# Seeding score banks with the mask: one column tile or two, by ScalarE alone or with VectorE

## The chip, the core and the metric

The kernel runs on one core of one Trainium2 chip. The metric is the time of one execution on the device in microseconds (us); the number compared is the median of several runs. A separate, profiled execution gives the trace. PE is TensorE's matmul part, PEld its weight loads, DVE is VectorE, ACT is ScalarE, POOL is GpSimd and SP is the SyncE queue that starts most DMAs. PSUM is the memory that matmuls write to, in eight banks of 128x512 f32.

## The reference, cut to what matters

The input x is 8 batches of 512 tokens with 256 features. Four layers follow one another, each added to x: a masked attention with 16 heads of 16 features, a mixture of 8 experts of which each token uses 2, and two linear maps. The change touches the attention:

```python
scores = jnp.einsum('bhsd,bhtd->bhst', q, k) * scale
scores = jnp.where(mask[None, None, :, :], -jnp.inf, scores)
attn = jax.nn.softmax(scores, axis=-1)
out = jnp.einsum('bhst,bhtd->bhsd', attn, v)
```

After it come an output projection, an RMS norm with gain and shift, the gate that picks two experts per token, and the experts.

## The kernel before, in words

The kernel first writes a list of steps, `order`, on the host; each engine then walks this one list and emits its own part of every step. Every engine therefore works in the order of the list, and waits are semaphores between engines.

**Groups and tiles.** Attention goes by groups: 4 heads of one batch, so 4 groups per batch and `GROUPS` = 32. The loop of `attention_order` runs over iterations i = 0 to 34, and inside over k = 0 to 3. One (i, k) is called a tile below. A tile holds, for n = 0 to 3, one `row` step and one `col` step. A `row` step multiplies queries by keys for 128 queries of group i (L1170), and DVE adds the mask and finds the maximum over the keys (L1643). These maxima are shared out again as extra rows of the queries (`split_maxima`, `maxima_rows`, and a small DMA, L984). A `col` step two iterations later computes the transposed scores of group i-2 for 128 keys, kt = k, of head hh = n, with the maximum already taken off (L1184). The mask must be added to them too. By default PE does that with a second matmul into the same bank, the identity times the mask (L1188). ACT then takes the exponential into `pt` (L1369).

**Seeds.** Where the list allows, the mask is in the bank before the scores are: ACT copies the mask there (L1375), and PE's score matmul adds onto it, without L1188. This is a seed. Before the change there is one per tile from group 1 on: 31 groups x 4 tiles = 124. `seed_after` says behind which exponential ACT makes it: two `col` steps ahead of the one that uses it (`SEED_AHEAD`). ACT must wait until the bank's last user has been read out.

**The ring.** Rows, columns and all side matmuls take seven banks in turn (`RING`). The user seven places earlier must have been read out before a bank is used again. With rows and columns alternating, the bank of a column was last that of a row. One side matmul in between makes it that of a column three places earlier.

**Side work.** `weigh` (the value products, L1203) stands in tiles with even k behind n = 2 and takes two key tiles at once. The other PE work of a batch waits in a list `todo`: 4 `project` (queries and keys of the next batch, L1147), 4 `project_v` (L1156) with 3 `stack` steps (DMAs that load the stacked parts of queries and keys), 4 `project_o` (L1221) and the `chain`. `work_off` takes one step of it at the end of each tile; it takes a `stack` step along with what stands before it. A chain is the norm, gate and routing of one batch as a generator: each of its yields is one n of a tile. It holds `scale` (DVE, L1692), `normalised` (POOL), the transposes `turn_x1`, squares (ACT, L1316), the gate, and `scatter` (POOL, indirect DMAs, L1980). Chains of later batches wait for earlier ones. In tiles of iterations 32 and 33 there are no rows, only columns.

**Weights for the experts.** Along the attention POOL splits expert weights into two parts in 64 chunks: SP fetches a chunk (L995), POOL splits it (L1879, L1881), SP stores it (L1000). `attention_over` lets the expert phase begin when the last chunk is stored. On SP's queue the last chunk's fetch stands behind `fetch_rows` (L1057), which waits for the scatters of batches 0 to 5.

**The expert phase** follows from about 615 us on, with matmuls at L1101. The diff does not touch its steps, but what is left of the last two chains runs in it.

Of the kernel before, what the change touches and what calls it, by code (L numbers as in the profile page):

```python
# [27 lines left out]
GROUPS = B * NG  # L28
# [19 lines left out]
SEED_AHEAD = 2  # L48
SHIFTS = 2
# [80 lines left out]
def chain(b, out):  # L130
# [10 lines left out]
    for st in range(ST):  # L141
        out.append(("scale", b, st))
        yield
# [7 lines left out]
    for st in range(ST):  # L151
        out.append(("square_x1", b, st))
        yield
# [95 lines left out]
def attention_order(out):  # L249
# [14 lines left out]
    def work_off():  # L264
        step = todo.pop(0)
        if step[0] == "chain":
            chains.append(chain(step[1], out))
        else:
            out.append(step)
            if step[0] == "project":  # L270
                rests.append(("rest",) + step[1:])
        if todo and todo[0][0] == "stack":
            work_off()
# [15 lines left out]
    for i in range(GROUPS + 3):  # L289
# [7 lines left out]
        for k in range(ST):  # L297
# [3 lines left out]
            for n in range(GH):  # L301
# [14 lines left out]
                if i * ST + k in FIRST_PROJECTS and n == 1 and i < 2:  # L316
                    work_off()
                if n == (3 if i < 2 else 0) and rests:
                    step = rests.pop(0)
                    out.append(step)  # L320
                    parted.append(("part",) + step[1:])
# [32 lines left out]
            for _ in range(2 if len(todo) > 12 else 1):  # L354
                if todo and i >= 2:
                    work_off()
# [83 lines left out]
def _build(nc, ctx, d, out):  # L440
# [323 lines left out]
    seed_after = {}  # L764
    for gi in range(1, GROUPS):
        for kt in range(ST):
            for hh in ((3, 2, 1, 0), (0, 1, 2, 3))[kt % 2]:
                place = col_place[gi, kt, hh]
                user = ring_before(("col", gi, kt, hh))
                if user[0] == "row" or user[0] == "col" and col_place[user[1:]] <= place - SEED_AHEAD:  # L770
                    seed_after[cols_at[place - SEED_AHEAD]] = gi, kt, hh
                    break
    seeded = signal("seeded", [seed_after[at] for at in cols_at if at in seed_after])
    project_place = {at: n for n, at in enumerate(projects)}
# [314 lines left out]
    def tensor_program(engine):  # L1089
# [49 lines left out]
        for step in order:  # L1139
# [32 lines left out]
            elif name == "col":  # L1172
# [3 lines left out]
                seed = (gi, kt, hh) in seeded.value  # L1176
                if seed:
                    pe.wait_ge(*seeded.at((gi, kt, hh)))
                else:
# [300 lines left out]
    def vector_program(engine):  # L1480
# [117 lines left out]
        for step in order:  # L1598
# [35 lines left out]
            elif name == "row":  # L1634
# [6 lines left out]
                if gi >= 2:  # L1641
                    dve.wait_ge(*max_split.at((gi - 2,)))
                V.tensor_tensor_reduce(junk[n % 2][:, :], ring_bank(step)[0][:, :], mneg[:, 0, st, :], 1.0, FLOOR, ALU.add, ALU.max,  # L1643
                                       rowmax[gi % 2][:, hh, st:st + 1]).then_inc(max_found.sem, 1)
            elif name == "split_maxima":
# [397 lines left out]
```

## Time and profile before

| what | value |
|---|---|
| median of 3 runs | 1162.13 us (1159.18 to 1162.16) |
| the profiled execution, its own time | 1156.71 us |
| its span from first to last instruction | 1154.8 us |
| mean granted TensorE clock | 0.991 of full speed |
| PE busy / DVE / ACT / POOL | 97% / 67% / 68% / 44% |

Busy time of PE is the union of matmul records whose ends are modelled: a 512-column matmul has a record of 0.38 us, but the next one starts 0.22 us later. Where PE is never short of work, the distance between starts is therefore its cost. All times in the trace are counted from the first instruction.

### The profile page before, as it was taken

The page shows a single profiled execution, that of the slowest core. Times are in us where ns is not written, and L with a number is a line of the kernel's source. Part 1 is how long each engine was busy: PE and PEld are TensorE (multiplying, and loading weights), DVE is VectorE, ACT ScalarE, POOL GpSimd, SP SyncE. Part 2 cuts the span into 40 slices and gives each one's busy share as a digit, 9 for nine tenths or more (in the row PEclk, how much of TensorE's full clock was granted, in tenths as well). Part 3 has the DMA queues.
Part 4 walks back from the last instruction along what each step waited for, and adds up shares of the span by engine and source line. Part 5 has one row for each costly group of instructions (what it writes and reads, how often), then busy time and mean ns, then how long its engine had stood idle before and what let it go on. Part 6 is the DMA issues. An engine that isn't in the chain of part 4 may idle for free.

```text
span 1154.8 us, 23346 instructions
## 1 busy us (share of the span) xinstructions
PE 1115.1 (97%) x7466; PEld 779.2 (67%) x7520; DVE 776.1 (67%) x2265; ACT 790.7 (68%) x1752; POOL 511.7 (44%) x837
## 2 busy tenths in 40 slices
PE   8899999999999999998988999999999999999988
PEld 5333434435344353443438989999999999999968
DVE  5877778787887878877745435356555555668647
ACT  2478778787787877866794656656566656666645
POOL 7424135584755837557552465354222222222210
PEclk8999999999999999998999999999999999999999
DMA  8765738367383663844737588846566666723536
GB/s 209 211 191 189 223 101 254 121 224 232 117 276 123 221 209 120 269 139 127 262 106 271 136 291 304 262 122 144 161 188 201 202 193 193 215 49 69 165 91 219
DMA packets 101616, 213.64 MB, mean 185 GB/s; under 512 B 10917, under 2 KB 71341, under 8 KB 93046
## 3 DMA queue, kind: packets, MB, share of 16 engines
q1 hardware_dynamic: 86038, 192.42, 51.3%
q0 software_dynamic: 14304, 18.69, 9.0%
q10 hardware_dynamic: 1152, 1.05, 0.4%
q8 instruction: 59, 0.97, 0.4%
q14 instruction: 63, 0.52, 0.1%
HBM read 239.28 MB, written 74.29 MB: 272 GB/s over the span
## 4 chain that ended last, share of the span: by engine, by line
PE 45%; POOL 2%; DMA 2%; DVE 2%; issue 1%; ACT 1%; SPq 1%; POOLq 0%; ACTq 0%
PE bank L1101 38%; PE bank L1261 1%; PE bank L1116 1%; DMA x<-yout,rows 1%; PE bank L1130 1%; PE bank L1203 1%; PE bank L1221 1%; POOL routed L1980 1%; DMA routed<-xw,idx 0%; PE bank L1295 0%; PE bank L1184 0%; PE bank L1170 0%; PE bank L1241 0%; DMA w_parts<-in_W 0%; POOL run L862 0%
## 5 line engine op out<-in xcount | busy, mean ns | idle before, releaser
L1643 DVE CUSTOM_DVE_ANT_0 junk<-bank,mneg 128x512 bf16<-128x512 f32 x512 | 332.5, 683 | 105.4 <-PE bank L1170 104.9
L1369 ACT ACTIVATE pt<-bank 128x512 f32<-128x512 f32 x512 | 300.9, 595 | 65.5 <-PE bank L1184 31.9
L1990 POOL DMA_INDIRECT x<-yout,rows x78 | 122.5, 1570 | 291.2 <-ACT yout L1453 231.1
L1101 PE MATMUL bank<-hid,w 128*128 128x256 f32 x1872 | 244.7, 287 | 3.9 <-DVE hid L1791 3.9
L1101 PEld LDWEIGHTS bank<-hid,w 128*128 128x128 f32 x1872 | 231.4, 191 | 5.6 <-issue 4.3
L1791 DVE TENSOR_TENSOR hid<-full,hid 128x256 fp32r<-128x256 f32 x312 | 133.1, 430 | 139.1 <-ACT full L1448 137.9
L1443 ACT ACTIVATE hid<-bank,biases 128x256 fp32r<-128x256 f32 x312 | 149.9, 480 | 93.2 <-PE bank L1101 91.3
L1448 ACT ACTIVATE full<-bank,biases 128x256 f32<-128x256 f32 x312 | 149.2, 478 | 0.0
L1188 PE MATMUL bank<-mneg,identb 128*128 128x512 bf16 x332 | 126.4, 381 | 0.0
L1203 PE MATMUL bank<-pt,vaug 128*17 128x512 f32 x1024 | 124.0, 602 | 1.4 <-DVE turned L1670 0.5
L1101 PE MATMUL bank<-w,hid 128*128 128x256 f32 x936 | 121.9, 283 | 1.5 <-DVE hid L1791 1.5
L1101 PE MATMUL bank<-rowsT,w 128*128 128x256 f32 x936 | 122.9, 284 | 0.2 <-DMA w<-split_weights 0.2
L1101 PEld LDWEIGHTS bank<-rowsT,w 128*128 128x128 f32 x936 | 116.0, 190 | 0.9 <-DVE rowsT L1782 0.7
L1101 PEld LDWEIGHTS bank<-w,hid 128*128 128x128 f32 x936 | 115.1, 190 | 1.7 <-issue 1.7
L1170 PE MATMUL bank<-stacks 96*128 96x512 bf16 x256 | 95.7, 389 | 8.0 <-DVE rest L1608 2.9
L1453 ACT ACTIVATE yout<-yout,rows 128x256 f32<-128x256 f32 x78 | 39.3, 508 | 92.5 <-DVE yout L1797 92.5
L1184 PE MATMUL bank<-qst,kst 98*128 98x512 bf16 x256 | 97.0, 382 | 5.5 <-DVE rowmax L1643 4.5
L1170 PE MATMUL bank<-kst,qst 96*128 96x512 bf16 x256 | 98.0, 383 | 2.4 <-DVE rowmax L1643 1.1
L1184 PE MATMUL bank<-stacks 98*128 98x512 bf16 x256 | 97.3, 380 | 2.7 <-DVE rowmax L1643 1.4
L1881 POOL TENSOR_TENSOR w_parts<-w_parts 128x512 fp32r<-128x512 f32 x64 | 81.6, 1274 | 5.2
L1375 ACT ACTIVATE bank<-mneg 128x512 f32<-128x512 bf16 x124 | 74.2, 598 | 8.5 <-DVE rowmax L1643 8.1
L1980 POOL DMA_INDIRECT routed<-xw,idx x64 | 64.3, 1005 | 17.1 <-issue 13.5
(184 smaller groups left out, 1455.0 us busy)
## 6 DMA issues: line engine op xcount, KB each, us to landing
w<-split_weights SPq DMA_DIRECT2D x80, 1024.0 KB
w<-split_weights SPq DMA_DIRECT2D x40, 2048.0 KB
split_weights<-w_parts SPq DMA_DIRECT2D x64, 512.0 KB, 3.8
w_parts<-in_W SPq DMA_DIRECT2D x64, 256.0 KB, 4.6
split_parts<-parts SPq DMA_DIRECT2D x28, 384.0 KB, 2.6
rows<-routed SPq DMA_DIRECT2D x39, 258.0 KB, 3.7
stacks<-split_parts SPq DMA_DIRECT2D x36, 256.0 KB, 5.5
qst<-split_parts SPq DMA_DIRECT2D x24, 256.0 KB, 5.2
```

The source lines that it names most:

```text
L1101: product = T.matmul(ps, w[p], x[q], start=(k == 0 and n == 0), stop=(k == len(weights) - 1 and n == 2))
L1170: T.matmul(ps[:, :], qst[b % 2][0:KQ, h, st * P:(st + 1) * P], kst[b % 2][0:KQ, h, :], start=True, stop=True).then_inc(row_scored.sem, 1)
L1184: product = T.matmul(ps[:, :], kst[b % 2][0:KQ + SHIFTS, h, kt * P:(kt + 1) * P], qst[b % 2][0:KQ + SHIFTS, h, :], start=not seed, stop=li ...
L1188: product = T.matmul(ps[:, :], identb[:, :], mneg[:, 1, kt, :], start=False, stop=True)
L1203: product = T.matmul(bank[5][32 * hh:32 * hh + D + 1, :], vaug[b % 2][:, kt, h, :], pt[col_place[gi, kt, hh] % len(pt)][:, :], start=(kt = ...
L1369: A.activation(pt[n % len(pt)][:, :], ps[:, :], ACT.Exp, scale=float(D) ** -0.5).then_inc(exped.sem, 1)
L1443: A.activation((hid1, hid2)[n - 1][j % 2][0][:, m, :], ps[:, 0:TW], ACT.Relu, bias=biases[j % NS][:, column:column + 1])
L1448: A.activation(full[place % len(full)][:, :], ps[:, 0:TW], ACT.Relu, bias=biases[j % NS][:, column:column + 1]).then_inc(rectified.sem, 1)
L1643: V.tensor_tensor_reduce(junk[n % 2][:, :], ring_bank(step)[0][:, :], mneg[:, 0, st, :], 1.0, FLOOR, ALU.add, ALU.max, rowmax[gi % 2][:, h ...
L1791: V.tensor_tensor(lo, h[:, :], hi.bitcast(F32), ALU.subtract).then_inc(hidden_low.sem, 1)
L1881: G.tensor_tensor(w_parts[n][:, 1], w_parts[n][:, 1].bitcast(F32), w_parts[n][:, 0].bitcast(F32), ALU.subtract).then_inc(w_low.sem, 1)
L1990: G.indirect_dma_start(x2_dram, bass.IndirectOffsetOnAxis(ap=rows[j % NS][:, tt, E + 1:E + 2].bitcast(U32), axis=0), yout[j % NY][:, tt], ...
```

## The change

It has two parts. The first makes two seeds per tile. In tiles with even kt, and in all tiles of the last two groups, ACT makes both. In tiles with odd kt of groups 1 to 29, ACT makes the first and DVE one more: behind the row maximum of the third row step before the column (`ROWS_AHEAD` = 3), if the bank's last user is far enough back. The order in which heads are tried changes too.

The second moves side work. From iteration 2 on, `work_off` is called only in tiles with odd k (those without `weigh`): at the tile's end, and also behind n = 1 unless the next step is a `project`. From iteration 30 on the end of every tile still calls it. A chain is now taken together with the step before it, so it begins earlier. For batches 0 to 4 the steps of `scale` and `square_x1` stand two yields apart instead of one.

```diff
+ROWS_AHEAD = 3
...
     for st in range(ST):
         out.append(("scale", b, st))
-        yield
+        for _ in range(2 if b < KNOWN - 1 else 1):
+            yield
...
     for st in range(ST):
         out.append(("square_x1", b, st))
-        yield
+        for _ in range(2 if b < KNOWN - 1 else 1):
+            yield
...
-        if todo and todo[0][0] == "stack":
+        if todo and todo[0][0] in ("stack", "chain"):
             work_off()
...
+                if k % 2 and n == 1 and i >= 2 and todo and todo[0][0] != "project":
+                    work_off()
...
-            for _ in range(2 if len(todo) > 12 else 1):
-                if todo and i >= 2:
-                    work_off()
+            if todo and i >= 2 and (k % 2 or i >= GROUPS - 2):
+                work_off()
...
-    seed_after = {}
+    rows_before, n = {}, 0
+    for step in order:
+        n += step[0] == "row"
+        if step[0] == "col":
+            rows_before[step[1:]] = n
+
+    def early(user, at):
+        if user[0] == "row":
+            return row_place[user[1:]] <= rows_before[at] - ROWS_AHEAD
+        return user[0] == "col" and col_place[user[1:]] <= col_place[at] - ROWS_AHEAD
+
+    seed_after, seed_behind = {}, {}
     for gi in range(1, GROUPS):
         for kt in range(ST):
-            for hh in ((3, 2, 1, 0), (0, 1, 2, 3))[kt % 2]:
-                place = col_place[gi, kt, hh]
+            by_vector = kt % 2 and gi < GROUPS - 2
+            free = []
+            for hh in ((3, 1, 2, 0), (0, 2, 1, 3))[kt % 2]:
                 user = ring_before(("col", gi, kt, hh))
-                if user[0] == "row" or user[0] == "col" and col_place[user[1:]] <= place - SEED_AHEAD:
-                    seed_after[cols_at[place - SEED_AHEAD]] = gi, kt, hh
-                    break
+                if user[0] == "row" or user[0] == "col" and col_place[user[1:]] <= col_place[gi, kt, hh] - SEED_AHEAD:
+                    free.append((gi, kt, hh))
+            for at in free[:1 if by_vector else 2]:
+                seed_after[cols_at[col_place[at] - SEED_AHEAD]] = at
+            for at in [at for at in free[1:] if by_vector and early(ring_before(("col", *at)), at)][:1]:
+                seed_behind[rows_at[rows_before[at] - ROWS_AHEAD]] = at
...
+                after = seed_behind.get((gi, hh, st))
+                if after:
+                    ps, freed = ring_bank(("col", *after))
+                    dve.wait_ge(masks_made, MASKS)
+                    dve.wait_ge(*freed)
+                    V.tensor_copy(ps[:, :], mneg[:, 1, after[1], :]).then_inc(seeded_too.sem, 1)
```

In the diff's last part, on DVE, the copy follows the row maximum at once. PE waits for `seeded_too` before the column that uses it.

## Rows read from the trace of the kernel before

**Rows 1.** The stages: us, busy time (instructions) of each engine, clock, DMA.
```profile
215.77:288.15 72.38, 71.86 (x391) 31.71 (x397) 58.98 (x172) 57.65 (x121) 45.71 (x92) 1.00 0.62 194
506.04:577.69 71.65, 65.34 (x361) 25.91 (x366) 56.01 (x171) 51.40 (x110) 45.13 (x99) 0.95 0.52 181
577.69:601.50 23.81, 20.80 (x125) 7.21 (x127) 11.23 (x41) 21.85 (x49) 16.33 (x34) 1.00 0.37 114
```

**Rows 2.** Waits of PE between 143.41 and 506.04 us, all of them.
```profile
PE bank L1170 <- DVE rowmax L1643: 0.8, 2, 0.4
```

**Rows 3.** Timeline of PE from tile (13, 0) to (13, 2): start, us.
```profile
236.55 0.38 PE L1170 MATMUL bank<-kst,qst 96*128 96x512 bf16 x1
...
240.89 0.38 PE L1170 MATMUL bank<-kst,qst 96*128 96x512 bf16 x1
...
242.20 0.38 PE L1184 MATMUL bank<-stacks 98*128 98x512 bf16 x1
...
243.52 0.38 PE L1170 MATMUL bank<-kst,qst 96*128 96x512 bf16 x1
```

**Rows 4.** Timeline of DVE in the same tile.
```profile
240.88 0.69 DVE L1643 CUSTOM_DVE_ANT_0 junk<-bank,mneg 128x512 bf16<-128x512 f32 x1 [0.16 <-PE bank L1170]
...
241.49 0.69 DVE L1643 CUSTOM_DVE_ANT_0 junk<-bank,mneg 128x512 bf16<-128x512 f32 x1
```

**Rows 5.** DVE groups by shape, whole span: us, mean ns of one.
```profile
L1692 DVE SCALAR_TENSOR_TENSOR osb<-osb,ssq,gain_shift 128x256 f32<-128x256 f32 x32 | 23.5, 736 | 1.3 <-POOL ssq L862 1.3
...
L1653 DVE CAST m<-rowmax 128x16 bf16<-128x16 f32 x32 | 12.1, 378 | 1.3 <-POOL below L1831 1.2
...
L1615 DVE MEMSET bank<- 128x512 f32 x1 | 0.5, 485 | 0.1
```

**Rows 6.** DVE groups by shape, 215.77 to 288.15 us.
```profile
L1655 DVE TENSOR_TENSOR m<-rowmax,m 128x16 bf16<-128x16 f32 x4 | 2.6, 651 | 0.1
```

**Rows 7.** Timeline of PE, tile (22, 1).
```profile
401.87 0.39 PE L1170 MATMUL bank<-kst,qst 96*128 96x512 bf16 x1 [0.40 <-DVE rowmax L1643]
```

**Rows 8.** Timeline of all engines around tile (30, 0).
```profile
537.97 1.56 DVE L1692 SCALAR_TENSOR_TENSOR osb<-osb,ssq,gain_shift 128x256 f32<-128x256 f32 x1
537.99 1.26 POOL L1881 TENSOR_TENSOR w_parts<-w_parts 128x512 fp32r<-128x512 f32 x1
...
540.20 0.61 PE L1184 MATMUL bank<-qst,kst 98*128 98x512 bf16 x1 [1.27 <-DVE rowmax L1643]
```

**Rows 9.** The same tile as a stage, columns as in rows 1.
```profile
537.14:547.06 9.92, 8.07 (x32) 1.96 (x31) 6.77 (x18) 3.65 (x7) 7.04 (x9) 0.66 0.54 159
```

**Rows 10.** ACT groups by shape, 577.69 to 601.50 us.
```profile
L1369 ACT ACTIVATE pt<-bank 128x512 f32<-128x512 f32 x31 | 16.9, 606 | 2.9 <-PE bank L1188 2.4 <-PE bank L1184 0.5
L1375 ACT ACTIVATE bank<-mneg 128x512 f32<-128x512 bf16 x8 | 4.9, 619 | 0.2 <-DVE rowmax L1643 0.2
L1316 ACT ACTIVATE squared<-osb 128x256 bf16<-128x256 f32 x4 | 1.7, 418 | 0.0
L1316 ACT ACTIVATION_READ_ACCUMULATOR squared<-osb 128x1 f32 x4 | 0.8, 203 | 0.0
```

**Rows 11.** The chain that ended last, end of attention: start, us.
```profile
591.91 2.43 DMA routed<-xw,idx
...
605.54 4.04 DMA w_parts<-in_W
...
611.87 2.62 DMA split_weights<-w_parts
```

**Rows 12.** SP's timeline there.
```profile
585.70 0.62 SPq L984 DMA_DIRECT2D qst<-mrow  x1
595.45 0.42 SPq L1057 DMA_DIRECT2D rows<-routed  x1
```

**Rows 13.** Waits of PE between 506.04 and 614.74 us: us in total, times, longest.
```profile
PE bank L1184 <- DVE rowmax L1643: 5.5, 6, 1.4
PE bank L1261 <- DMA split_weights<-w_parts: 4.6, 1, 4.6
```

More of the change, by code:

```diff
@@ L762, in ring_before @@
         return ring_users[n] if n >= 0 else None
-    seed_after = {}
+    rows_before, n = {}, 0
[8 more added lines that the diff above has]
+    seed_after, seed_behind = {}, {}
     for gi in range(1, GROUPS):
         for kt in range(ST):
-            for hh in ((3, 2, 1, 0), (0, 1, 2, 3))[kt % 2]:
-                place = col_place[gi, kt, hh]
+            by_vector = kt % 2 and gi < GROUPS - 2
+            free = []
+            for hh in ((3, 1, 2, 0), (0, 2, 1, 3))[kt % 2]:
                 user = ring_before(("col", gi, kt, hh))
-                if user[0] == "row" or user[0] == "col" and col_place[user[1:]] <= place - SEED_AHEAD:
-                    seed_after[cols_at[place - SEED_AHEAD]] = gi, kt, hh
-                    break
+                if user[0] == "row" or user[0] == "col" and col_place[user[1:]] <= col_place[gi, kt, hh] - SEED_AHEAD:
[4 more added lines that the diff above has]
+                seed_behind[rows_at[rows_before[at] - ROWS_AHEAD]] = at
     seeded = signal("seeded", [seed_after[at] for at in cols_at if at in seed_after])
+    seeded_too = signal("seeded_too", [seed_behind[at] for at in rows_at if at in seed_behind])
     project_place = {at: n for n, at in enumerate(projects)}
@@ L1175, in tensor_program @@
                 ps, freed = ring_bank(step)
-                seed = (gi, kt, hh) in seeded.value
-                if seed:
+                seed = (gi, kt, hh) in seeded.value or (gi, kt, hh) in seeded_too.value
+                if (gi, kt, hh) in seeded.value:
                     pe.wait_ge(*seeded.at((gi, kt, hh)))
+                elif seed:
+                    pe.wait_ge(*seeded_too.at((gi, kt, hh)))
                 else:
```

## The prediction

> **What bounds the kernel now.** I read the stages first, because PE's 97% is a union of modelled records and says little. In a batch period of attention the engines other than PE have slack: of 72.38 us DVE is busy 58.98 and ACT 57.65 [rows 1]. Then the waits: in 362.6 us of steady attention PE waits 0.8 us in all [rows 2]. The timeline shows what that means. Six 512-column matmuls lie between the starts at 240.89 and 242.20, so one costs 1.31 / 6 = 0.218 us, and a whole tile without side work takes 2.63 us [rows 3]. Iterations 4 to 27 are bound by PE alone, and a matmul taken from PE there gives 0.218 us, if nothing else becomes late. At the end it is different. In iterations 28 to 31 (506.04 to 577.69) PE waits for DVE and its clock falls for a while; in 32 and 33 ACT is busy 21.85 of 23.81 us [rows 1]. Then PE waits 4.6 us for the last chunk of expert weights [rows 13].
>
> **Term 1, the masks.** The old rule makes 124 seeds. By ring arithmetic two banks of four are nearly always allowed: the new rule makes 62 x 2 (even kt), 58 + 8 (odd kt) by ACT, and 58 by DVE. 248 seeds take 124 more mask matmuls off PE. Eight stand in iterations 32 and 33, where PE isn't the bound. 116 x 0.218 = 25.3 us come off. This is all of the gain that the edit aims at, 2.2% of the time.
>
> **Term 2, the wait for DVE's seeds.** ACT's second seed in an even tile is behind a column after which PE still has the value products or the next side work; I cost it at nothing in iterations 4 to 31. ACT gets 8 x 0.6 = 4.8 us more per batch and stays at 62.5 of some 72; if its cover goes, a wait of that length shows up. DVE's seed is closer. Take an odd tile without a step behind n = 1, row 0 starting at t = 0. PE issues row 0, column 0 (seeded by ACT), row 1, column 1, its mask, row 2, and wants column 2 at 6 x 0.218 = 1.31. That column is DVE's (order 0, 2, 1, 3: the first free is ACT's, the next DVE's), and its copy is behind row 0. In tile (13, 1) the row 0 started on PE at 240.89 and its maximum on DVE at 241.49, 0.60 later, held by the maximum before; two maxima start 0.61 apart [rows 3, 4]. So the copy starts at 1.21. Its length is on no row. Nearest below is DVE's memset of a bank, 0.485, which reads nothing; nearest above is the maximum itself, 0.69, which reads a bank and the mask [rows 4, 5]. I take 0.65, near the top, as it reads a source. The copy ends at 1.86, PE goes on at about 1.92 (0.06 for the semaphore, an estimate), so it stands 0.61 us. Between the bounds it is 0.45 to 0.65. Queued behind PE's wait are all its later matmuls; nothing later in the tile gives the time back.
>
> Where a side step stands behind n = 1 (0.87 us for a value or output tile), column 2 is wanted at 2.18, and the wait is gone. So I count tiles: the four `project` of a batch are at the head in the odd tiles of iterations i with i mod 4 = 0 and 1, which have no step behind n = 1: 24 tiles for six batches. Iterations 28 and 29 have no side work: 4. (30, 1), (31, 1), (31, 3): 3. Iteration 3: 2. That is 33 of 58 odd tiles: 33 x 0.61 = 20.1 us, and the other 25 at nothing. Four masks per group give 0.87 us; two such tiles take back 1.2. (Bounds: 33 x 0.45 = 14.9 to 33 x 0.65 = 21.5.)
>
> **Term 3, DVE late.** The wait assumes that DVE is level with PE. `scale` steps now fall on calls 12, 14, 16 and 18 of a chain: two in tile (12, 3), two in (13, 0) (and every four iterations). In (13, 0) DVE has four maxima at 0.61, `split_maxima` at about 0.35 + 0.65, a `rest` at 0.6, and two `scale` at 0.74: 5.5 us [rows 4 to 6], where PE needs 4.34 [rows 3] less one mask, 4.12. Something of this is hidden by the value products. I carry 1.0 us into (13, 1), a tile of term 2, whose wait becomes 1.6. Five chains: +5.0. Before, the four `scale` stood in one tile and cost PE one such wait per chain, as in tile (22, 1), 0.40 [rows 7]; x 5 this goes: -2.0.
>
> **Term 4, iterations 28 to 31.** Chain 5 now begins at (28, 0) and not at (28, 3). Its four `scale` stay one n apart. Before, one took 1.56 us beside a POOL split of 1.26, PE waited 1.27 at once, and the clock was at half right after it (0.61 for a record of 0.38) [rows 8]; tile (30, 0) took 9.92 us at clock 0.66 [rows 9], some 5 more than the 4.34 of [rows 3] with its transpose. The same pile-up comes three tiles earlier behind a bare tile. I take -3 (that the clock holds), with +3 as the other end.
>
> **Term 5, iterations 32 and 33.** Eight tiles get one more ACT copy. ACT starts an exponential every 0.61 us there and is the bound: 8 x 0.61 = +4.9. But chain 6 now begins in iteration 31, so four squares of 0.418 + 0.203 leave this stretch: -2.5 [rows 10]. Net +2.4.
>
> **Term 6, the last chunk.** SP issues `fetch_rows` at 595.45, right after the scatters of chain 5 land (591.91 + 2.43). Its `mrow` DMA before it went at 585.70, so it stood for over 9 us. The chunk's fetch (605.54), split and store (to 614.5) hang on that [rows 11, 12]. Chain 5 ends 13 calls of n, over three tiles, earlier, so SP no longer stands, and the store ends at about 605, before PE wants it. The 4.6 us of [rows 13] go: -4.6. If chain 5 isn't earlier by 5 us, 0.
>
> **The other moves** I cost at nothing. The last `stack` DMAs are issued half a tile to one tile later, with four tiles to go before the rows that need them. The mask DMAs, chunk order and the expert phase's steps stay; PE there keeps its work. `maxima_rows` keeps its place on SP, and the `part` DMAs in front of it move by a tile or more behind POOL; their cover is the three tiles until the columns.
>
> **Sum.** -25.3 + 20.1 + 5.0 - 2.0 - 3.0 + 2.4 - 4.6 = -7.4 us. From the profiled 1156.7 (span 1154.8 and 1.9 around it) this gives 1149.3. The median of the runs is 5.4 above the profiled one; I carry the difference over: 1162.1 - 7.4 = 1154.7.
>
> **A rule beside the rows.** DVE's casts `m<-rowmax` and the `scale` steps show what a busy POOL can do: a mean of 378 and 736 ns, and one of 1.56 us beside a POOL operation [rows 5, 8]. If the seeds were held like that, the wait would grow. The Trainium skill, page "SBUF — State Buffer", section "Who interferes with whom", says that a VectorE instruction with one SBUF input outside the two-port modes does not contend with GpSimd, and its page "VectorE: DVE Perf Modes" keeps the two-port modes to SBUF operands. By this rule the copy into PSUM is never held and the sum stays; no run here shows it yet.
>
> **Rivals.**
> 1. *The masks' gain arrives whole.* DVE would be level, the copy at its lower bound, and PE delayed elsewhere so that 1.31 stretches. For it: PE waited 0.8 us in all [rows 2]. Against: the distances of [rows 3, 4] leave no room. With half of the waits: -25.3 + 10 - 2 - 3 - 4.6 + 2.4 + 2 = -20; with none -32, 1130. Chance 0.18.
> 2. *Held copies (slower).* POOL holds each of the 58 copies by 0.4 us on average, as the casts (0.378 against 0.2 at best) and `scale` suggest. In the 33 tiles that adds 0.4 each, in the other 25, with 0.27 to spare, 0.2, and what DVE is late is passed on to the ACT seeds that wait for maxima: 13 + 5 + some 4 = 22, so +15 in all, 1177. It turns slower from 0.22 us per seed in the 33 tiles on (7.4 / 33). Chance 0.15.
> 3. *The clock falls.* A wait of 1.6 us in one tile, five times, each followed by half clock as in [rows 8, 9], where about 6.8 us at half cost 3.4: +17, so +10, 1172. For it: [rows 8]. Against: PE there had several waits in a row. [...] Chance 0.07.
> 4. *Even.* Term 6 or term 4 doesn't come, or DVE is later than 1.0: -3.5 to +3.5. Chance 0.18.
>
> **Numbers.** My own case, -3.5 to -15, has 0.42. A measurement of this kernel tells about 0.3%, 3.5 us, from no change. Faster 0.42 + 0.18 = 0.60; same 0.18; slower 0.22. The range holds 8 in 10 from the better half of rival 1 to below rival 2: 1136 to 1171. My case's own range is 1147 to 1159.
>
> **What would show it.** L1188 falls by 124 (some records missing). A DVE copy bank<-mneg x58 appears at 0.6 to 0.7 us. PE waits on it in some 33 tiles, 0.6 each, and the tiles (i mod 4 = 1, k = 1) are the longest of their kind. Batch periods are 72 us, not 69. PE's 4.6 us wait for the chunk is gone, and fetch_rows is issued some 9 us after less waiting. ACT's L1375 is x190. I'm wrong if the periods are 69 (DVE's seeds in time) or above 74 (held copies or clock), or if the copies are well under 0.5 us.

## The result and the profile after

The median after is 1163.08 us (1160.83 to 1166.23, 20 runs), that of before 1160.2 us (1156.03 to 1163.11, 20 runs). The ratio is 1.0026, with a 95% interval of 1.0016 to 1.0035: slower by 3 us, which is clear of its interval but within the 0.3% that the prediction calls no change, where 7.4 us less were forecast. The profiled execution has a span of 1159.2 us (before 1154.8) at a mean clock of 0.992. Two executions of those below, of 2240 us (the kernel before) and 3863 us (the profiled one of kernel 11), were disturbed ones and stand in no ratio. Stretches of two profiled executions are compared by their lengths. Whole kernels are compared by their ratios to the kernel before on the same chip, since that kernel itself takes 1155.2 us on one chip used here and 1160.2 on another.

The edit does what it says. First the groups of the whole span, by shape, of ACT, PE and DVE: by the code 124 mask matmuls are gone (388 before, 264 after, of which the trace holds 215), ACT makes 190 seeds, DVE 58 at 0.69 us each.

```profile
L1397 ACT ACTIVATE bank<-mneg 128x512 f32<-128x512 bf16 x190 | 113.9, 599 | 28.7 <-DVE rowmax L1665 25.9
...
L1210 PE MATMUL bank<-mneg,identb 128*128 128x512 bf16 x215 | 82.1, 382 | 0.0
```

```profile
L1672 DVE CAST bank<-mneg 128x512 f32<-128x512 bf16 x58 | 40.0, 689 | 0.0
```

The stages: the batch period that answers to [rows 1] (iterations 12 to 15), iterations 28 to 31, iteration 31 alone, and iterations 32 and 33 to the last column. Columns as in [rows 1].

```profile
214.88:288.03 73.15, 69.29 (x375) 30.07 (x380) 60.74 (x179) 61.06 (x130) 45.32 (x92) 1.00 0.62 192
506.69:582.04 75.35, 63.66 (x344) 24.17 (x349) 62.65 (x201) 56.31 (x125) 47.65 (x103) 0.93 0.52 183
557.54:582.04 24.50, 18.11 (x81) 5.81 (x81) 18.41 (x67) 14.02 (x32) 15.59 (x33) 0.79 0.56 212
582.04:608.90 26.86, 19.46 (x117) 5.76 (x118) 8.05 (x18) 25.12 (x50) 9.23 (x18) 1.00 0.38 119
```

A period was 72.38 and is 73.15: PE is busy 2.6 us less in it and the time doesn't fall. That is the first thing to see: the matmuls came off, and waits took their place. Next the waits of PE, from 142.4 to 506.7 us (they answer to [rows 2]) and from there to 620 us ([rows 13]):

```profile
PE bank L1206 <- DVE bank L1672: 10.4, 20, 0.9
PE bank L1190 <- DVE rowmax L1665: 3.3, 4, 0.8
PE bank L1190 <- ACT logits L1430: 1.7, 5, 0.3
```

```profile
PE bank L1206 <- ACT bank L1397: 9.6, 12, 1.2
PE bank L1190 <- DVE rowmax L1665: 4.8, 6, 2.1
PE bank L1206 <- DVE bank L1672: 4.3, 6, 1.5
```

The wait for the last chunk of weights (4.6 us in [rows 13]) is gone. SP's timeline shows how: `fetch_rows` now goes out 2.0 us behind `mrow`, not 9.75 [rows 12], and the chunk's fetch is issued 2.9 us earlier than in [rows 11]. The last column comes 7.6 us later (608.90, before 601.28), so part of this wait went because PE itself arrives later:

```profile
590.55 0.62 SPq L1004 DMA_DIRECT2D qst<-mrow  x1
592.55 0.42 SPq L1077 DMA_DIRECT2D rows<-routed  x1
...
602.65 0.43 SPq L1015 DMA_DIRECT2D w_parts<-in_W  x1
```

**The close seed.** PE and DVE in tile (5, 1), an odd tile with a `project` and no step of a chain:

```profile
97.10 0.38 PE L1190 MATMUL bank<-kst,qst 96*128 96x512 bf16 x1
...
98.19 0.38 PE L1190 MATMUL bank<-kst,qst 96*128 96x512 bf16 x1
99.05 0.39 PE L1206 MATMUL bank<-stacks 98*128 98x512 bf16 x1 [0.48 <-DVE bank L1672]
```

```profile
97.69 0.69 DVE L1665 CUSTOM_DVE_ANT_0 junk<-bank,mneg 128x512 bf16<-128x512 f32 x1
98.31 0.08 DVE L1665 DVE_READ_ACCUMULATOR2_ANT rowmax<- 128x1 f32 x1
98.31 0.69 DVE L1672 CAST bank<-mneg 128x512 f32<-128x512 bf16 x1
```

The row starts at 98.19 and column 2 could follow at 98.41. It starts at 99.05, 0.64 later: the copy runs from 98.31 to 99.00. (The wait shown, 0.48, counts from the modelled end of the last record; the distance between starts is the cost.) Over the batches, such tiles with k = 1 take 4.83 us, and with k = 3 4.55. In kernel 3 below, where PE adds this mask itself, they take 4.40 and 4.12. Less one matmul of 0.218 that is 4.18 and 3.90, so PE stands for 0.65 us in both, and such a seed costs 0.43 net. In value and output tiles it stands for nothing: 4.19 and 3.91 for kernel 3's 4.40 and 4.12.

**The scale steps.** DVE and POOL before and in tile (13, 0):

```profile
230.73 1.35 DVE L1720 SCALAR_TENSOR_TENSOR osb<-osb,ssq,gain_shift 128x256 f32<-128x256 f32 x1 [0.87 <-POOL ssq L882]
...
233.23 0.96 DVE L1720 SCALAR_TENSOR_TENSOR osb<-osb,ssq,gain_shift 128x256 f32<-128x256 f32 x1
...
236.28 0.47 DVE L1720 SCALAR_TENSOR_TENSOR osb<-osb,ssq,gain_shift 128x256 f32<-128x256 f32 x1
```

```profile
230.50 0.20 POOL L882 TENSOR_TENSOR ssq<-ssq 128x4 f32<-128x4 f32 x1
230.65 1.16 POOL L1876 TENSOR_TENSOR parts<-rest,parts 128x512 bf16<-128x512 f32 x1
231.75 0.81 POOL L1907 CAST w_parts<-w_parts 128x512 fp32r<-128x512 f32 x1
232.64 1.27 POOL L1909 TENSOR_TENSOR w_parts<-w_parts 128x512 fp32r<-128x512 f32 x1
```

DVE first waits 0.87 us for the last of POOL's norm operations, with row maxima queued behind, and then its first two scales take 1.35 and 0.96 us beside POOL's splits, the third 0.47. Tile (13, 0) takes 5.15 us and (13, 1) 5.23, where 4.13 and 4.83 stand in chains without this. Four chains (1 to 4) show it alike; chain 0, whose first scale comes at 158.28 and takes 0.47, loses nothing.

**Iteration 31** takes 24.50 us at a clock of 0.79 (before: 17.17 us). PE from its wait in tile (31, 0) on, then DVE:

```profile
562.43 0.39 PE L1206 MATMUL bank<-qst,kst 98*128 98x512 bf16 x1 [0.82 <-ACT bank L1397]
...
564.12 0.39 PE L1190 MATMUL bank<-kst,qst 96*128 96x512 bf16 x1 [0.43 <-DVE rowmax L1665]
...
565.50 0.39 PE L1190 MATMUL bank<-kst,qst 96*128 96x512 bf16 x1 [0.77 <-DVE rowmax L1665]
...
567.27 0.39 PE L1190 MATMUL bank<-kst,qst 96*128 96x512 bf16 x1 [0.94 <-DVE rowmax L1665]
568.48 0.61 PE L1206 MATMUL bank<-qst,kst 98*128 98x512 bf16 x1 [0.83 <-DVE bank L1672]
...
573.76 0.61 PE L1190 MATMUL bank<-kst,qst 96*128 96x512 bf16 x1 [2.11 <-DVE rowmax L1665]
```

```profile
560.28 0.17 DVE L882 CAST tbi<-run 128x8 int32<-128x8 f32 x1 [2.88 <-POOL gt L882]
...
565.36 0.29 DVE L882 TENSOR_TENSOR tj<-flts,tv 128x128 f32<-128x128 f32 x1
565.68 0.29 DVE L882 TENSOR_TENSOR tj<-tj,tb 128x128 f32<-128x128 f32 x1
566.01 0.29 DVE L882 TENSOR_REDUCE tv<-tj 128x16 f32<-128x128 f32 x1
566.33 0.18 DVE L882 TENSOR_TENSOR tv<-flts,tv 128x16 f32<-128x16 f32 x1
...
566.52 0.68 DVE L1665 CUSTOM_DVE_ANT_0 junk<-bank,mneg 128x512 bf16<-128x512 f32 x1
```

These small DVE operations build the routing table of chain 5. They run from 560.28 to 573.07, in front of row maxima and between them; before they ran from 575.46 to 585.55, where the rows ended at 577.69. Ahead of the first DVE is idle for 2.88 us until POOL is done, though PE had started the matmul of the next row maximum at 557.54. PE waits five times in a row, and from 568.48 a record is 0.61 and not 0.38. That is half clock, 1.2 GHz, which the trace shows for 10.2 us.

**Iterations 32 and 33.** ACT by shape, 582.04 to 608.90 us: twice as many seeds as in [rows 10], and ACT is busy 25.12 of 26.86 us.

```profile
L1391 ACT ACTIVATE pt<-bank 128x512 f32<-128x512 f32 x32 | 18.1, 594 | 2.0 <-PE bank L1206 1.9
L1397 ACT ACTIVATE bank<-mneg 128x512 f32<-128x512 bf16 x16 | 9.6, 601 | 0.0
```

### The profile page after: what moved, and what is told of

It is laid out like the page before. It is cut to its first block, busy times and chain, and to the rows that moved or that the text cites. A ratio compares the mean times of both kernels' runs of the same rounds, so it can differ in the third digit from the quotient of the medians.

```text
span 1159.2 us, 23216 instructions
## 1 busy us (share of the span) xinstructions
PE 1092.7 (94%) x7349; PEld 762.4 (66%) x7396; DVE 794.0 (68%) x2323; ACT 818.3 (71%) x1818; POOL 508.0 (44%) x837
## 4 chain that ended last, share of the span: by engine, by line
PE 47%; DVE 4%; POOL 3%; ACT 3%; issue 3%; another core or an unknown queue 1%; DMA 0%; POOLq 0%; ACTq 0%; DVEq 0%
PE bank L1121 37%; PE bank L1225 2%; PE bank L1283 1%; PE bank L1206 1%; PE bank L1136 1%; DVE junk L1665 1%; PE bank L1190 1%; ACT pt L1391 1%; PE bank L1150 1%; POOL routed L2008 1%; DVE hid L1819 1%; PE bank L1263 1%; POOL xin L882 1%; PE bank L1317 0%
## 5 line engine op out<-in xcount | busy, mean ns | idle before, releaser
L1665 DVE CUSTOM_DVE_ANT_0 junk<-bank,mneg 128x512 bf16<-128x512 f32 x512 | 334.3, 684 | 75.6 <-PE bank L1190 72.2
L1391 ACT ACTIVATE pt<-bank 128x512 f32<-128x512 f32 x512 | 290.0, 592 | 51.8 <-PE bank L1206 33.5
L1121 PE MATMUL bank<-hid,w 128*128 128x256 f32 x1872 | 243.5, 287 | 3.9 <-DVE hid L1819 3.9
L1121 PEld LDWEIGHTS bank<-hid,w 128*128 128x128 f32 x1872 | 230.3, 191 | 5.8 <-issue 3.6
L1397 ACT ACTIVATE bank<-mneg 128x512 f32<-128x512 bf16 x190 | 113.9, 599 | 28.7 <-DVE rowmax L1665 25.9
L1121 PE MATMUL bank<-w,hid 128*128 128x256 f32 x936 | 122.3, 284 | 2.4 <-DVE hid L1819 2.4
L1121 PE MATMUL bank<-rowsT,w 128*128 128x256 f32 x936 | 123.4, 284 | 0.0
L1121 PEld LDWEIGHTS bank<-w,hid 128*128 128x128 f32 x936 | 115.3, 190 | 2.8 <-issue 2.7
L1121 PEld LDWEIGHTS bank<-rowsT,w 128*128 128x128 f32 x936 | 116.2, 190 | 0.2
L1876 POOL TENSOR_TENSOR parts<-rest,parts 128x512 bf16<-128x512 f32 x32 | 38.1, 1192 | 112.4 <-ACT parts L1361 112.4
L1210 PE MATMUL bank<-mneg,identb 128*128 128x512 bf16 x215 | 82.1, 382 | 0.0
```

The source lines that it names most:

```text
L1121: product = T.matmul(ps, w[p], x[q], start=(k == 0 and n == 0), stop=(k == len(weights) - 1 and n == 2))
L1391: A.activation(pt[n % len(pt)][:, :], ps[:, :], ACT.Exp, scale=float(D) ** -0.5).then_inc(exped.sem, 1)
L1397: A.activation(ps[:, :], mneg[:, 1, after[1], :], ACT.Copy).then_inc(seeded.sem, 1)
```

## The experiments

All were timed against the kernel before on the same chip. Kernels 1 to 4 shared one chip, 5 to 8 another, 9 to 11 a third, and kernel 12 ran on a fourth. Stage lengths are those of each profiled execution, in us:

| kernel | ratio (95%) | to 28 | period 12-15 | 28-31 | 32-last col. | behind | span |
|---|---|---|---|---|---|---|---|
| before | 1 | 506.0 | 72.4 | 71.7 | 23.6 | 553.5 | 1154.8 |
| after | 1.0026 (1.0016-1.0035) | 506.7 | 73.2 | 75.4 | 26.9 | 550.3 | 1159.2 |
| 1 seeds only | 1.0168 (1.0154-1.0182) | 524.4 | 74.8 | 72.3 | 30.4 | 547.9 | 1174.9 |
| 2 order only | 0.9906 (0.9888-0.9923) | 504.1 | 72.2 | 72.5 | 20.7 | 549.9 | 1147.2 |
| 3 no DVE seeds | 0.9962 (0.9949-0.9974) | 501.0 | 72.1 | 71.6 | 26.9 | 548.4 | 1147.9 |
| 4 DVE seeds a row earlier | 0.9944 (0.9931-0.9957) | 499.6 | 71.7 | 76.0 | 26.9 | 548.7 | 1151.2 |
| 5 one seed at the end | 1.0014 (0.9999-1.0029) | 507.4 | 73.2 | 76.0 | 20.7 | 549.8 | 1153.9 |
| 6 only far DVE seeds | 0.9939 (0.9921-0.9957) | 498.5 | 71.9 | 74.4 | 26.9 | 546.4 | 1146.2 |
| 7 seeds where free | 0.987 (0.985-0.989) | 496.0 | 71.4 | 70.5 | 20.7 | 548.7 | 1135.8 |
| 8 chain 5 late | 0.9932 (0.9917-0.9947) | 503.9 | 72.2 | 63.5 | 26.3 | 551.0 | 1144.7 |
| 9 scales later | 0.9975 (0.9956-0.9993) | 503.2 | 71.6 | 76.4 | 26.9 | 549.4 | 1155.8 |
| 10 = 7 + 9 | 0.9809 (0.9786-0.9831) | 491.4 | 70.2 | 73.3 | 20.7 | 548.5 | 1134.0 |
| 11 = 7, chain 5 at 17 | 0.9816 (0.9792-0.9839) | - | - | - | - | - | - |
| 12 = 10 + 11 | 0.9763 (0.9739-0.9787) | 490.2 | 70.1 | 68.6 | 21.4 | 543.9 | 1124.0 |

Kernel 11 has no usable profile, so no stages. Within iterations 4 to 27 the batches show more than one period does. Here is the time from the first row of a batch's iterations to that of the next, in us:

| kernel | 4 to 7 | 8 to 11 | 12 to 15 |
|---|---|---|---|
| before | 68.90 | 72.37 | 72.37 |
| 2 order only | 68.86 | 72.06 | 72.19 |
| 3 no DVE seeds | 67.59 | 70.53 | 72.11 |
| after | 68.54 | 71.50 | 73.15 |
| 9 scales later | 68.54 | 71.52 | 71.64 |

**1. Seeds alone, 2. order alone.** Kernel 1 has the seeds of the change on the order of before; kernel 2 the order of the change with one ACT seed per tile as before.

```diff
 kernel 1, against after:
-        for _ in range(2 if b < KNOWN - 1 else 1):
-            yield
+        yield
...
-        if todo and todo[0][0] in ("stack", "chain"):
+        if todo and todo[0][0] == "stack":
...
-                if k % 2 and n == 1 and i >= 2 and todo and todo[0][0] != "project":
-                    work_off()
...
-            if todo and i >= 2 and (k % 2 or i >= GROUPS - 2):
-                work_off()
+            for _ in range(2 if len(todo) > 12 else 1):
+                if todo and i >= 2:
+                    work_off()
```

```diff
 kernel 2, against after:
-            for at in free[:1 if by_vector else 2]:
-                seed_after[cols_at[col_place[at] - SEED_AHEAD]] = at
-            for at in [at for at in free[1:] if by_vector and early(ring_before(("col", *at)), at)][:1]:
-                seed_behind[rows_at[rows_before[at] - ROWS_AHEAD]] = at
+                    seed_after[cols_at[place - SEED_AHEAD]] = gi, kt, hh
+                    break
```

> The second seed per tile, with the list of steps of the kernel before (side work at the end of every tile). Theory A (each DVE seed that is wanted 1.3 us after its row costs PE 0.6 to 0.7 us, whatever the load): the old list has no step behind n = 1, so nearly all 58 DVE seeds come late: 58 x 0.65 = 38 us against 27 us of masks, so some 10 us slower than before, L1672 waited for by PE in 50 or more tiles. Theory B (the mean load of DVE and ACT, not the distance, eats the gain): as the changed kernel, +3 us. Rival C (the new list of steps is what costs time, the seeds gain): 5 to 25 us faster than before.

> The new list of steps with the seeds of the kernel before (one per tile, by ACT). Theory A: PE is the bound in iterations 4 to 27 and has the same work, so nothing there (0 to -2 us); at the end the wait for the last chunk (4.6 us) goes. So 3 to 6 us faster than before, if iterations 28 to 31 cost no more than before. Rival C (the order costs): slower than before by 2 us or more, with the loss in iteration 31, where the table steps of batch 5 now stand in front of row maxima.

Measured: seeds alone cost 1.7%, 19.4 us where theory A had 10, and the order alone gives 0.94%, 10.9 us where 3 to 6 were expected. The two aren't independent. Seeds on the old order cost 19.4 us, on the new one 1.0026 - 0.9906 = 1.20%, 13.9 us. Kernel 1's waits of PE up to 615 us:

```profile
PE bank L1203 <- DVE bank L1669: 23.9, 46, 2.7
PE bank L1203 <- ACT bank L1394: 14.2, 29, 1.5
```

There both kinds of seed are late, DVE's 46 times. So the order is needed for these seeds, but it is the whole of the gain, and the seeds spend it.

**3. No seeds by DVE, 4. DVE's seeds one row earlier, 6. only the far ones.** Three ways at the same question: is it the distance between the copy and its column?

```diff
 kernel 3:
-            for at in [at for at in free[1:] if by_vector and early(ring_before(("col", *at)), at)][:1]:
+            for at in []:
 kernel 4:
-ROWS_AHEAD = 3
+ROWS_AHEAD = 4
 kernel 6:
+    def apart(at):
+        return ring_place[("col", *at)] - ring_place[("row", *rows_at[rows_before[at] - ROWS_AHEAD])]
...
-            for at in [at for at in free[1:] if by_vector and early(ring_before(("col", *at)), at)][:1]:
+            for at in [at for at in free[1:] if by_vector and early(ring_before(("col", *at)), at) and apart(at) > 5][:1]:
```

> The changed kernel without DVE's seeds: ACT's 190 stay, the 58 columns get their mask from PE again. Theory A: PE gets 58 x 0.218 = 12.6 us of masks and loses its waits on L1672 (17.7 us by the trace) and part of those on late row maxima: 5 to 12 us faster than the changed kernel. Batch periods near 70.7 us. Theory B: DVE is freed of 58 x 0.6 us, ACT still loaded: gain of up to 5 us. If ACT's second seeds were what costs, it stays at the changed kernel's time plus 5 to 12.

> The changed kernel with ROWS_AHEAD = 4: DVE copies one row maximum earlier (57 seeds). Theory A: the copy ends about 0.6 us earlier against PE, so the wait in the 33 tiles falls from 0.6-0.7 to 0-0.1 us: 15 to 22 us faster than the changed kernel, batch periods 69 to 70 us. Theory B (load): same copies, same load, so within 3 us of the changed kernel.

> The changed kernel with DVE's seeds only where a side matmul stands between row 0 and the column that uses it (26 of 58). The other 32 get their mask on PE. If each close seed costs PE 0.65 us: 32 x (0.65 - 0.22) = 14 us faster than the changed kernel, and also faster than the kernel without any DVE seed by up to 26 x 0.22 = 5.6 us. If the wait is made up for elsewhere: 0 to 7 us.

Measured: without DVE's seeds 0.64% less than after, 7.4 us. With 57 of them, one row earlier, 0.82% less, 9.5 us, where 15 to 22 were expected; with the 26 that have a side matmul before their column 0.87% less, 10 us for 14. Kernel 4's tiles with a `project` take 4.50 and 4.23 us: PE stands for 0.33 in them, half of the 0.65 and not the 0 to 0.1 expected, which is still 0.11 more than the mask gives. Kernel 4's waits of PE up to 615 us, one row of them:

```profile
PE bank L1206 <- DVE bank L1672: 2.6, 5, 1.0
```

In kernel 6 the same tiles take 4.40 and 4.12, which is their matmuls with the mask put back, and no wait for a DVE seed is left between 74 and 498 us. The distance is shown to be the cause of the close seeds' loss, and the length of the copy is the same in all (0.69). But a far seed gives only its 0.22.

Kernel 3 shows something else too. Against kernel 2 it has ACT's second seeds alone. They give 1.27 and 1.53 us of the 1.74 (8 x 0.218) in the first two batches of the table, and 0.08 in iterations 12 to 15. There (12, 3) and (13, 0) take 4.67 and 5.14 us, where kernel 2 has 4.12 and 4.48: the scale steps. The first scale of kernel 2, then that of kernel 3:

```profile
229.96 1.35 DVE L1695 SCALAR_TENSOR_TENSOR osb<-osb,ssq,gain_shift 128x256 f32<-128x256 f32 x1
```

```profile
227.93 1.35 DVE L1720 SCALAR_TENSOR_TENSOR osb<-osb,ssq,gain_shift 128x256 f32<-128x256 f32 x1 [1.36 <-POOL ssq L882]
```

Kernel 2 has the two long scales as well (1.35 and 0.95), and its (13, 0) is only 0.13 longer than the 4.35 without them. What differs is DVE's wait for POOL's norm: at most 0.15 us in kernel 2, 0.87 in after, 1.36 in kernel 3. From the start of (12, 3), POOL's norm ends at 1.4 us in kernel 2 and at 2.7 in after. Masks taken off PE bring the rows forward and not POOL's work.

**5. One ACT seed per tile in the last two groups.**

```diff
-            for at in free[:1 if by_vector else 2]:
+            for at in free[:1 if by_vector or gi >= GROUPS - 2 else 2]:
```

> The changed kernel with one seed per tile, as before, for the last two groups (iterations 32 and 33; 182 ACT seeds, 58 DVE seeds). If ACT bounds these two iterations, eight copies of 0.61 us go: 4 to 5 us faster than the changed kernel, and the time from iteration 32 to the last column falls from 26.9 to about 22 us. If PE or POOL bounded them, no change or up to 1.7 us slower (8 masks).

Measured: the stretch falls from 26.9 to 20.7, more than the 22 expected. The ratio falls only from 1.0026 to 1.0014, some 1.4 us with an interval that reaches from a gain of 3 to a loss of 1, where 4 to 5 were expected. The profiled executions keep 5.3 us of the 6.2, but they stand on two chips, and the kernel before is 5.0 us faster on that of kernel 5. In kernel 5's, 1.3 us come back before the 48th matmul of L1121 (9.37 after the last column, not 8.10), and 0.7 in iterations 28 to 31, which this edit hardly touches. So what the edit is worth as a whole stays open; kernels 7, 10, 11 and 12 keep it.

**8. Chain 5 late.** Kernel 2 with the pause between chain 5's `residual` and its first `scale` 24 calls long and not 11.

```diff
-    for _ in range({KNOWN - 1: 11, KNOWN: 16, B - 1: 6}.get(b, 8)):
+    for _ in range({KNOWN - 1: 24, KNOWN: 16, B - 1: 6}.get(b, 8)):
```

> The new list of steps with the seeds of before, and chain 5 held back by 13 calls (pause of 24 in place of 11), so that its gate, table and scatters stand where they stood before. If the early table steps in front of row maxima are what makes iteration 31 long: it falls from 24 to about 17 us; the wait for the last chunk comes back (4 to 5 us), as do chain 6's squares in iterations 32 and 33 (2.5 us). Net 0 to 3 us slower than the new list alone. If the early chain gains more than that, 6 us or more slower.

Measured, iterations 28 to 31 and iteration 31 as stages; PE's wait for the chunk:

```profile
503.86:567.38 63.52, 61.95 (x366) 25.98 (x365) 51.83 (x159) 51.41 (x109) 35.04 (x78) 1.00 0.57 198
551.24:567.38 16.14, 14.98 (x88) 5.74 (x87) 11.77 (x42) 11.76 (x24) 8.02 (x22) 1.00 0.61 233
```

```profile
PE bank L1264 <- DMA split_weights<-w_parts: 4.2, 1, 4.2
```

The stage is 9.0 us shorter than kernel 2's 72.5, at full clock throughout: chain 5's steps among the rows cost that much. But 5.7 us return in iterations 32 and 33, and 1.1 behind, where the chunk is waited for again, and the ratio is 0.26% worse than kernel 2's. The two ends pull against each other; kernel 8 went too far.

**9 and 10. Scales later.** The pause before the scales of chains 0 to 4 ten calls and not eight, the one behind them three and not five; on after (9) and on kernel 7 (10). The expectations name chains 0 to 3; the edit also reaches chain 4, and the four chains that can gain are 1 to 4.

```diff
-    for _ in range({KNOWN - 1: 11, KNOWN: 16, B - 1: 6}.get(b, 8)):
+    for _ in range({KNOWN - 1: 11, KNOWN: 16, B - 1: 6}.get(b, 10)):
...
-    for _ in range({KNOWN - 1: 3, B - 1: 10}.get(b, 5)):
+    for _ in range({KNOWN - 1: 3, B - 1: 10, KNOWN: 5}.get(b, 3)):
```

> The kernel after, with the pause between the residual and the first scale of chains 0 to 3 ten calls long and not eight, and the pause behind the last scale three and not five (chains 4 and 5 as they are). The scale steps then stand one tile later, behind the parts and split_weights operations of POOL. Theory: the tile (13, 0) and its like take 5.1 us and not 4.13 because DVE first waits for POOL's ssq (0.87) and is then held (1.35 and 0.96 us for scale operations that take 0.47 alone); with the steps later the four chains lose less: (12, 3) back from 4.78 to 4.55, (13, 0) from 5.15 to about 4.2, (13, 1) from 5.23 to 4.83; 1.2 to 1.6 us per chain, 4 chains, 5 to 6 us faster than the kernel after, ratio to before 0.997 to 0.998. Rival: DVE is late merely because it has two more operations of 0.74 in a tile, wherever they stand: then the loss moves one tile on with the steps and the time is that of the kernel after, ratio 1.002.

> The fastest kernel so far (second seeds only where they are free: 174 by ScalarE, 24 by VectorE) with the same edit of the pauses. Theory (POOL holds the scale steps): (12, 3) from 4.86 to 4.12 and (13, 0) from 5.15 to about 4.2, some 1.5 us for each of four chains: ratio to before 0.982. Rival (the loss moves with the steps): 0.987 as without the edit.

Measured: 0.51% and 0.61% less. Kernel 9's four scales in DVE's timeline, the first three being those shown above for after:

```profile
232.73 1.13 DVE L1720 SCALAR_TENSOR_TENSOR osb<-osb,ssq,gain_shift 128x256 f32<-128x256 f32 x1
236.50 0.48 DVE L1720 SCALAR_TENSOR_TENSOR osb<-osb,ssq,gain_shift 128x256 f32<-128x256 f32 x1
238.11 0.48 DVE L1720 SCALAR_TENSOR_TENSOR osb<-osb,ssq,gain_shift 128x256 f32<-128x256 f32 x1
240.32 0.48 DVE L1720 SCALAR_TENSOR_TENSOR osb<-osb,ssq,gain_shift 128x256 f32<-128x256 f32 x1
```

Tile (12, 3) is back at 4.55, (13, 0) at 4.13, and (13, 1) falls to 4.96; a scale of 1.13 is still there, the wait for POOL is not. The loss doesn't move along with the steps, so it was the meeting with POOL and not merely two more operations. From iteration 4 to 27 the profiled executions differ by 5.3 us.

**7. Second seeds only where they are free.** DVE's in odd tiles with a side step before column 2, one row earlier; ACT's only in even tiles; one seed per tile in the last six groups. 174 by ACT, 24 by DVE.

```diff
-ROWS_AHEAD = 3
+ROWS_AHEAD = 4
...
+    def side_between(gi, kt):
+        return ring_place["col", gi, kt, 2] - ring_place["col", gi, kt, 1] > 2
...
-            by_vector = kt % 2 and gi < GROUPS - 2
+            by_vector = kt % 2 and gi < GROUPS - 6 and side_between(gi, kt)
...
-            for at in free[:1 if by_vector else 2]:
+            for at in free[:2 if kt % 2 == 0 and gi < GROUPS - 6 else 1]:
```

> The new list of steps; second ACT seeds in tiles with even kt only up to group 25, DVE seeds (24) one row earlier and only with a side matmul in between, one seed per tile from group 26 on (iterations 28 to 33 as with the new list of steps alone). Expected against that kernel: 50 + 24 masks x 0.218 = 16 us less, less 5 to 6 us that chains cost where scale waits for POOL: 10 us faster than it, ratio to before about 0.982. If ACT's second seeds cost in general, it is no faster than the new list alone (0.9906).

Measured: 0.987, 15 us less than before, where 0.982 was expected. Against kernel 2 that is 0.36% by the ratios, 4 us and not 10; by the profiled executions, on two chips, it is 11.4, 8.1 of them before iteration 28.

**11 and 12. Chain 5's pause 17 calls**, on kernel 7 and on kernel 10 (`KNOWN - 1: 11` becomes `KNOWN - 1: 17`).

> The fastest kernel so far with chain 5's pause behind its residual 17 calls long and not 11. With 24 calls (under the old seeds) iteration 31 fell from 23.8 to 16.1 us but the wait for the last chunk of weights came back at 4.2 us and rows came late. Theory of the two ends: chain 5's table steps cost PE and the clock in iteration 31 if they stand there (+8), and the chunk's wait comes back if chain 5 ends later than about 595 us. Six calls are 1.5 tiles of odd and even, some 9 us of time: iteration 31 falls by 2 to 5 us, the chunk wait stays under 2: ratio 0.984 (0.981 to 0.988). Rival: the half clock comes from the scale steps and not from the table steps, so moving them changes which tile is slow and not how much: 0.987.

> The last two edits together: second seeds where they are free, scale steps of chains 0 to 3 two calls later, chain 5's pause 17 calls and not 11. If the two gains are independent, as the theory has them in different stretches (chains 0 to 3 before 506 us, chain 5 behind it), the ratios multiply: 0.9809 * 0.9816 / 0.987 = 0.9755, time about 1130 us, and iteration 31 takes under 20 us where it took 22.4, with the wait for the last chunk under 2 us. Rival: chain 5 later only moves work behind the last column, 0.981.

Measured: 0.9816 and 0.9763, where 0.9755 was the product. Kernel 12's median is 1128.95 us (before, on its chip, 1156.36), the fastest here. Iterations 28 to 31 fall by 4.8 us against kernel 10 (whose stage is 2.9 longer than kernel 7's, which wasn't traced), and there is no wait for the chunk; behind the last column another 4.6 are gone, which I didn't trace. Iteration 31 takes 20.9 us, not under 20, at a clock of 0.92:

```profile
537.96:558.81 20.85, 16.98 (x87) 5.64 (x86) 17.80 (x71) 12.37 (x25) 13.76 (x30) 0.92 0.59 227
```

## Why the prediction was off

Two steps failed. Term 3 priced the scale steps by DVE's busy time and left out that DVE waits for POOL in front of them. Term 4 moved the same steps earlier in iterations 28 to 31 and forgot the rest of the chain, whose table lands in front of row maxima. Term 2, the close seeds, was right.

The forecast splits into the order's terms (the old scale waits -2.0, term 4, the squares of term 5, term 6: -12.1 us) and the seeds' (-25.3 + 20.1 + 5.0 + 4.9 = +4.7). Kernel 2 splits the measurement in the same way. In us, by spans:

| stretch | order: forecast | measured | seeds: forecast | measured |
|---|---|---|---|---|
| to iteration 28 | -2.0 | -2.0 | -0.9 | +2.6 |
| 28 to 31 | -3.0 | +0.9 | +0.8 | +2.8 |
| 32 to the last column | -2.5 | -2.9 | +4.9 | +6.2 |
| behind | -4.6 | -3.6 | 0 | +0.4 |
| sum | -12.1 | -7.6 | +4.7 | +12.0 |

(The seeds' share of a stretch in the forecast is 0.218 per mask and 0.61 per close tile in it, and term 3's +5.0. By the ratios the order gives -10.9 and the seeds +13.9; the profiled execution of kernel 2 was 3 us above its median, and on another chip.) Seen as one sum, the four stretches are off by +3.5, +5.9, +0.9 and +1.4.

- **Term 1** held in most tiles: an even tile takes 4.13 us, in kernel 2 4.35, and a value or output tile 4.19 for 4.40. I had priced every mask taken off as if its tile ended with PE. In iterations 12 to 15 kernel 3 gets 0.22 in six of the eight even tiles, 1.3 us in all, and nothing in (14, 2). It loses 1.2 of that in (12, 3) and (13, 0), where the scales are.
- The order's -2.0 came (kernel 2, -2.0 between iterations 4 and 27). I had taken it from a single wait of 0.40 times five, where [rows 2] has only 0.8 in all. The tile lengths before show most of it: 4.14 in (22, 1) and (26, 1), 3.75 in (10, 1) and 3.70 in (14, 1), where (18, 1) takes 3.54, 1.6 us together. That the sum came so near is luck.
- **Term 2** was right. In tile (5, 1) the copy starts 1.21 us behind row 0 and column 2 at 1.95 (forecast 1.21 and 1.92); the copy takes 0.69 (taken 0.65, bound 0.69), and PE stands for 0.65 (taken 0.61) in the tiles named. For the semaphore I had put 0.06, from no row; from the copy's end to the column's start it is 0.05 (99.00 to 99.05). Kernel 3 gives 7.4 us for DVE's seeds; the forecast has 20.1 - 58 x 0.218 = 7.5.
- **Term 3 was mis-sized, and for another reason than its own.** The step read "I carry 1.0 us into (13, 1)", with scales at 0.74 and no wait for POOL. The trace has 1.35 and 0.96 for the first two scales and a wait of 0.87 for POOL before them, and kernel 2, with the long scales and hardly a wait, loses 0.13. Such waits were there to be read: [rows 5] has 1.3 us of them, for `ssq`, in the whole span before. The loss is 1.0 us in (13, 0), which I had assumed level with PE, and another 0.4 in (13, 1), 1.4 per chain. It falls on four chains, not five: 5.8 with the 0.2 of (12, 3), for 5.0. Kernel 9 takes all but a rest in (13, 1) away, 5.9 us by the ratio and 5.3 by the tiles.
- **No term had** what comes on top of that. (14, 2) and (15, 2), and their like in five batches, give nothing for their masks, and (15, 2) is 0.05 longer: 0.5 per batch, 2.4 in all. Kernel 9 has it too, so it isn't the scales'. (15, 2) is back at 4.13 in kernel 7, with its copies a row earlier and fewer of them; (14, 2) isn't explained.
- **Term 4 failed**, and is the largest miss. The step was "The same pile-up comes three tiles earlier behind a bare tile. I take -3 (that the clock holds), with +3 as the other end". The scales' pile-up in iteration 30 did shrink (tile (30, 0) takes 6.05 us, not 9.92). But I moved only the scales in my mind. The chain's later steps move too, and its table, which stood where the rows end, now stands 15 us earlier, in iteration 31 in front of maxima: 24.50 us for 17.17. The stage is +3.7 where -2.2 was forecast. In kernel 2, without the seeds, iteration 31 takes 23.8 us as well. The seeds add 2.8 to the stage, for 0.8: tile (29, 1) alone takes 5.22 for kernel 2's 4.09, with a wait of 1.48 for its copy. Kernel 8 shows that chain 5's place is the cause: with it later the stage is 9.0 us shorter than in kernel 2, 7.7 of them in iteration 31, and the clock stays full. Kernel 8 moves the scales together with the table; that the table makes the waits is read from the timeline above, and no run moves it alone.
- **Term 5** was +3.3 for +2.4, and **term 6** came (the wait is gone, SP as described) but behind the last column only 3.2 of 4.6 us are gained. Kernel 2, where the last column is early (597.3) and the wait is gone too, shows that an earlier chain 5 is enough for it.
- **The rivals.** The whole gain (1) didn't come: the close seeds stand. The held copies (2) didn't either: the 58 copies take 0.685 to 0.695 us, and 37 of them overlap an operation of POOL, DMAs not counted. The Trainium skill, page "SBUF — State Buffer", section "Who interferes with whom", has no contention with GpSimd for a VectorE instruction with one SBUF input; the trace agrees with 0.69. The clock (3) fell for 10.2 us in iteration 31, behind several waits in a row. Behind single ones, of up to 0.9 us in steady attention and one of 1.48 at 529.39, it stayed at 1.00. What happened is the even case (4), which had 0.18, with its two reasons, "term 4 doesn't come" and "DVE is later than 1.0".

## What to carry over

Before pricing a matmul taken from the bounding engine, list per tile what ends next if it goes. In this kernel a second seed by DVE gives 0.22 us in a tile where a side step stands between the copy and its column, and costs 0.43 in one without. One by ACT gives 0.22, but not in the tiles where DVE waits for POOL. Look at waits between the other engines as well as at their busy time: less work on PE doesn't bring POOL forward. When a chain of steps starts earlier, follow its last steps as well as its first ones to the tiles where they land. Placing was worth more than removing: as the kernels were built up, the order gave 0.9%, the later scales 0.6% and chain 5's pause 0.5% of the 2.4% of kernel 12, the seeds 0.4%.

## What was not expected of the hardware

The same DVE copy into PSUM takes 0.69 us whatever POOL does here, while a DVE operation with two inputs in SBUF takes 1.35 us beside POOL for 0.47 alone. Not every overlap does that: chain 0's first scale takes 0.47 from 158.28 on, though a cast of POOL ends at 158.41 and a split starts at 158.49. What decides it isn't shown. Here is a seed beside a POOL split, DVE and POOL in tile (13, 3):

```profile
249.22 0.69 DVE L1672 CAST bank<-mneg 128x512 f32<-128x512 bf16 x1
```

```profile
249.30 1.27 POOL L1909 TENSOR_TENSOR w_parts<-w_parts 128x512 fp32r<-128x512 f32 x1
```

The granted clock stayed at its upper level, 2.4 GHz, through single waits of up to 0.9 us in steady attention and one of 1.48 us in iteration 29; with the five waits of 0.43 to 0.94 us from 562.43 to 568.48 it fell to the lower one, 1.2 GHz, for 10.2 us.
